# One-hot rows of a graph kernel's gate stage, written as four-byte words in two passes

## The reference, cut to what matters

```python
ei = emb[atom_z[src]]
ej = emb[atom_z[dst]]
gate = gate + (ei * (ej @ adapt)).sum(-1, keepdims=True)
msg = gate * h[dst] * (cw * mj)[:, None]
agg = jax.ops.segment_sum(msg, src, num_segments=N)
```

## Time and profile before

| | us |
|---|---|
| median of three runs | 5722.47 |
| lowest, highest | 5720.83, 5742.07 |
| the profiled execution | 5716.15 |
| its span | 5714.5 |
| the gate stage in it, some 1201 to 1871 | 670 |

### The profile page before, as it was taken

One profiled execution on the slowest core, in us unless ns is written; L12 is line 12 of the kernel. 1 busy time (PEld: TensorE's weight loads), 2 busy tenths in 40 slices (PEclk: granted clock), 3 DMA queues, 4 the chain that ended last, 5 costly groups with the idle time before them and its releaser, 6 DMA issues. The chain is left out here.

```text
span 5714.5 us, 186702 instructions
## 1 busy us (share of the span) xinstructions
PE 4266.2 (75%) x79491; PEld 3587.6 (63%) x79576; DVE 3792.0 (66%) x7929; ACT 2244.4 (39%) x7754; POOL 2676.4 (47%) x2702
## 2 busy tenths in 40 slices
PE   6888884036666499859976997699757844978887
PEld 3555542035665389848875887588636733977786
DVE  6888875069999588667766875677585446545244
ACT  3333331036666255535543554455402424101310
POOL 2777777756666177627752775367421510000000
PEclk7766665569889699979987998799787977988897
DMA  9322222257676344344424442444155443000000
GB/s 353 79 74 73 69 68 65 53 130 205 191 203 184 115 156 155 111 109 164 155 93 122 167 158 74 137 163 166 55 103 211 146 120 110 2 9 4 4 4 10
DMA packets 480761, 652.89 MB, mean 114 GB/s; under 512 B 315713, under 2 KB 362949, under 8 KB 476694
## 3 DMA queue, kind: packets, MB, share of 16 engines
q1 hardware_dynamic: 443541, 591.08, 33.0%
q0 software_dynamic: 33856, 48.44, 3.5%
q10 hardware_dynamic: 2496, 0.98, 0.1%
HBM read 460.24 MB, written 180.09 MB: 112 GB/s over the span
## 5 line engine op out<-in xcount | busy, mean ns | idle before, releaser
L299 POOL DMA_INDIRECT edges<-sb_bk_rec,sb_bk_pos x782 | 783.5, 1002 | 324.9 <-issue 235.0
L1718 ACT ACTIVATE sb_at_val<-banks,sb_at_prob 128x49 f32<-128x49 f32 x3800 | 772.2, 324 | 189.9 <-PE banks L1654 182.4
L1757 DVE TENSOR_REDUCE sb_at_tops<-banks 128x1 f32<-128x512 f32 x1000 | 653.3, 662 | 275.7 <-PE banks L1634 272.9
L1610 PE MATMUL banks<-sb_near,sb_at_hotT_d 128*128 128x49 bf16 x11100 | 609.8, 184 | 36.4 <-issue 18.6
L1612 PE MATMUL banks<-sb_queryp,sb_at_hotT_s 128*128 128x49 bf16 x11400 | 624.3, 185 | 14.1 <-issue 13.9
L1570 POOL TENSOR_TENSOR sb_at_key<-sb_at_key,sb_at_attr 128x400 f32<-128x400 f32 (+1 forms) x400 | 371.3, 929 | 498.2 <-ACT sb_at_key L1702 487.2
L1610 PEld LDWEIGHTS banks<-sb_near,sb_at_hotT_d 128*128 128x128 fp8e4 x11100 | 559.8, 96 | 41.5 <-issue 34.5
L1612 PEld LDWEIGHTS banks<-sb_queryp,sb_at_hotT_s 128*128 128x128 fp8e4 x11400 | 559.8, 96 | 17.1 <-issue 17.0
L1577 POOL TENSOR_TENSOR sb_at_val<-sb_at_val 128x490 f32<-128x490 f32 (+1 forms) x400 | 386.7, 967 | 68.3 <-ACT sb_at_val L1718 66.8
L1579 POOL TENSOR_TENSOR sb_at_val<-sb_at_val 128x490 f32<-128x490 f32 (+1 forms) x400 | 386.1, 965 | 31.3
L1654 PE MATMUL banks<-sb_near,sb_at_hotT_d 128*128 128x49 bf16 x11100 | 358.8, 186 | 35.7 <-ACT sb_at_val L1718 22.6
(11 more groups left out here) (695 smaller groups left out, 10114.5 us busy)
## 6 DMA issues: line engine op xcount, KB each, us to landing
sb_at_attr<-attr SPq DMA_DIRECT2D x100, 760.0 KB, 7.5
sb_at_hotT_s<-rows_src_t SPq DMA_DIRECT2D x100, 608.0 KB, 5.2
sb_at_hot_s<-rows_src SPq DMA_DIRECT2D x100, 608.0 KB, 8.7
sb_at_hotT_d<-rows_dst_t SPq DMA_DIRECT2D x100, 592.0 KB, 6.1
edges<-sb_pad SPq DMA_DIRECT2D x95, 460.0 KB
sb_gt_rec<-edges SPq DMA_DIRECT2D x25, 1748.0 KB
sb_we_hotT<-rows_dst_t SPq DMA_DIRECT2D x52, 592.0 KB, 5.7
attr<-sb_gt_rec SPq DMA_DIRECT2D x25, 760.0 KB, 12.7
```

The costliest lines, as they stand in the source:

```text
L299: pool.indirect_dma_start(list1, bass.IndirectOffsetOnAxis(pos[:, t:t + 1], 0), rec[:, k, j, :], None).then_inc(sent[k], 16)
L1610: pe.matmul(ps[:, 0, H1 * j:H1 * j + H1], where, what, start=(n == 0), stop=(n == 2))
L1718: ins = act.mul(val[:, v % VB, j, 0, :], ps[:, 5, H1 * j:H1 * j + H1], prob[:, i % 2, k:k + 1])
L1757: dve.tensor_reduce(tops[:, i % 2, g:g + 1], ps[:, 3 + x % 2, 0:P * len(RG[g])], AX, ALU.max).then_inc(s_top, 1)
```

## The change

Four fp8 numbers fill one 32-bit word, so a row of 128 columns is 32 words. Only one of them isn't zero, and its value is the fp8 one (56) moved to one of four bytes. `at_nodes` works out each place's quarter (its number divided by four) and its word's value (from the number's last two bits), in four more instructions that each wait for the one before. A piece is then made by two instructions: `same_quarter` compares 32 numbers with the place's quarter and writes bf16 zeros and ones into `same` (two buffers), and `one_hots` multiplies these with the word, read as fp32, and writes int32 into the memory of the one-hots. `same_quarter` stands in the unit where the comparison stood, ahead of `message(u)`; `one_hots` stands behind `message(u)`. What is written for PE and the stores is byte for byte what it was.

```diff
-                dve.tensor_scalar(ls[:, at, :], rec[:, i % HB, :, R_SRC], -float(P * i), None, ALU.add).then_inc(s_at, 1)
-                dve.tensor_tensor(ld[:, at, :], rec[:, i % HB, :, R_DST], starts, ALU.subtract).then_inc(s_at, 1)
+                dve.tensor_scalar(loc[:, 0, :], rec[:, i % HB, :, R_SRC], -float(P * i), None, ALU.add).then_inc(s_at, 1)
+                dve.tensor_tensor(loc[:, 1, :], rec[:, i % HB, :, R_DST], starts, ALU.subtract).then_inc(s_at, 1)
...
+                link(dve.tensor_scalar(byte[:], loc[:], 3, None, ALU.bitwise_and))
+                link(dve.tensor_scalar(word[:, at], byte[:], float(2 ** 26), float(531 * 2 ** 21), ALU.mult, ALU.add))
+                link(dve.tensor_scalar(loc[:], loc[:], 2, None, ALU.arith_shift_right))
+                link(dve.tensor_copy(quarter[:, at], loc[:]))
...
-                dve.tensor_tensor(to[:, i % HB, a:b, :], along(c["iota"][:], b - a), bc(loc[:, i % 2, a:b], P), ALU.is_equal,
-                                  saturate=False).then_inc(s_hot, 1)
...
+                    dve.tensor_tensor(same[:, m % 2, 0:b - a, :], along(c["iota"][:, 0:W4], b - a),
+                                      bc(quarter[:, i % 2, v, a:b], W4), ALU.is_equal).then_inc(s_same, 1)
...
+                    dve.wait_ge(s_same, m + 1)
+                    to = (hot_s if side == "s" else hot_d)[:, i % HB, a:b, :].bitcast(I32)
+                    dve.tensor_tensor(to, same[:, m % 2, 0:b - a, :], bc(word[:, i % 2, v, a:b].bitcast(F32), W4), ALU.mult
+                                      ).then_inc(s_hot, 1)
...
-            for n in range(NM):
-                one_hot(0, n)
+            for n in range(0, NM, 2):
+                same_quarter(0, range(n, n + 2))
+                one_hots(0, range(n, n + 2))
...
-                        for n in MAKE_AT[q]:
-                            one_hot(i + 1, n)
+                        same_quarter(i + 1, MAKE_AT[q])
                     message(u)
+                    if i + 1 < NB:
+                        one_hots(i + 1, MAKE_AT[q])
```

More of the change, by code:

```diff
@@ L1237, in gate_edges @@
     rec = m.sb("gt_rec", [P, HB, KT, REC])
-    ls, ld = m.sb("gt_ls", [P, 2, KT]), m.sb("gt_ld", [P, 2, KT])
+    W4 = P // 4
+    loc, byte = m.sb("gt_loc", [P, 2, KT], I32), m.sb("gt_byte", [P, 2, KT], I32)
+    quarter, word = m.sb("gt_quarter", [P, 2, 2, KT]), m.sb("gt_word", [P, 2, 2, KT], I32)
+    same = m.sb("gt_same", [P, 2, 12, W4], BF16)
     hot_s, hot_d = m.sb("gt_hot_s", [P, HB, KT, P], F8), m.sb("gt_hot_d", [P, HB, NW, P], F8)
@@ L1247, in gate_edges @@
     names = ["near", "at", "hot", "turned", "copied", "rows", "emb", "prod", "msg", "rest", "split2", "sum", "added",
-             "link", "second", "back"]
+             "link", "second", "back", "same"]
     with stage(nc, "gate", *names, *[f"rec{k}" for k in range(HB)], *[f"outh{k}" for k in range(HB)], "outt0", "outt1",
@@ L1251, in gate_edges @@
             block, s_near, s_at, s_hot, s_turned, s_copied, s_rows, s_emb, s_prod, s_msg, s_rest, s_split2, s_sum,
-            s_added, s_link, s_second, s_back, *dmas):
+            s_added, s_link, s_second, s_back, s_same, *dmas):
         s_rec, s_outh, s_outt, s_outa, s_far = dmas[0:3], dmas[3:6], dmas[6:8], dmas[8:11], dmas[11:15]
@@ L1429, in at_nodes, with same_quarter, one_hots @@
                 dve.tensor_tensor(w1[:, i, :], rec[:, i % HB, :, R_W1], dead[:, i, :], ALU.add).then_inc(s_at, 1)
[L1431 to L1436, removed]
-                dve.tensor_tensor(to[:, i % HB, a:b, :], along(c["iota"][:], b - a), bc(loc[:, i % 2, a:b], P), ALU.is_equal,
-                                  saturate=False).then_inc(s_hot, 1)
+                link(dve.tensor_scalar(byte[:], loc[:], 3, None, ALU.bitwise_and))
+                link(dve.tensor_scalar(word[:, at], byte[:], float(2 ** 26), float(531 * 2 ** 21), ALU.mult, ALU.add))
+                link(dve.tensor_scalar(loc[:], loc[:], 2, None, ALU.arith_shift_right))
+                link(dve.tensor_copy(quarter[:, at], loc[:]))
+            def same_quarter(i, ns):
+                for n in ns:
+                    side, a, b = MAKE[n]
+                    m, v = NM * i + n, "sd".index(side)
+                    if m >= 2:
+                        dve.wait_ge(s_hot, m - 1)
+                    dve.tensor_tensor(same[:, m % 2, 0:b - a, :], along(c["iota"][:, 0:W4], b - a),
+                                      bc(quarter[:, i % 2, v, a:b], W4), ALU.is_equal).then_inc(s_same, 1)
+            def one_hots(i, ns):
+                for n in ns:
+                    side, a, b = MAKE[n]
+                    m, v = NM * i + n, "sd".index(side)
+                    if n == 0 and i >= HB:
+                        dve.wait_ge(s_outh[i % HB], 32 * (i // HB))
+                        dve.wait_ge(s_sum, Q * (i - HB + 1))
+                    dve.wait_ge(s_same, m + 1)
+                    to = (hot_s if side == "s" else hot_d)[:, i % HB, a:b, :].bitcast(I32)
+                    dve.tensor_tensor(to, same[:, m % 2, 0:b - a, :], bc(word[:, i % 2, v, a:b].bitcast(F32), W4), ALU.mult
+                                      ).then_inc(s_hot, 1)
             def message(u):
```

## The result

The changed kernel takes 6182.8 us (median of four runs, 6180.1 to 6190.0) where the kernel before takes 5724.4 (median of four), a ratio of 1.079 with a 95% interval of 1.078 to 1.081. The forecast was 6142, with a range of 6010 to 6200.

The account below looks back on a forecast made before the run. A one-unit ring through PE, ACT and DVE was to bound the gate stage: 38.8 us a block plus 0.75 x 6.7 for the clock gives 43.8 against 26.3; 24 blocks add 420, plus 2 once: 6142 us, range 6010 to 6200.

Parts of the forecast that it names:

- Part 1, the ring of one unit: Gate stage: piece finished behind its message, so PE, ACT and DVE wait in turn each unit; 38.8 us a block against 26.3.
- L: Gate stage: way from a finished piece through PE to the end of ACT's multiplications; 3.03 to 3.82 us at 2.4 GHz.
- my 2.6: Lower end of the forecast wait of DVE's message for ACT in nearly every gate-stage unit, some 2.6 to 4 us.
- Part 2, the product: DVE's two short passes for one long: product 0.41 to 0.59 us on the ring; bounds -30 and +60 us in all.
- sign of failure: Gate-stage pieces: the prediction was to fail if the two-pass piece took over 1 us.
- Part 3, the nodes' step: Four more instructions in `at_nodes`, 0.9 us a block, hidden in q = 0's wait: cost 0, except 2 us once.
- The clock: PE's granted clock in the gate stage: three quarters of units at 1.2 GHz, raising a block from 38.8 to 43.8 us.
- the possible 6.7: Extra us a gate-stage block if PE's clock were 1.2 GHz throughout, 45.5 against 38.8.
- first rival, the low clock in every unit: Gate stage: PE's pauses return the clock to half in every unit, 45.5 us a block, 6185 us; chance 0.19.
- The rival on the other side: Gate stage: DVE's work alone sets the pace, so shorter pieces save 4.4 us a block, 105 us: 5617; chance 0.04.

Follow-up runs that it names:

- the kernel with the product early and short splits: The changed kernel with the product ahead of message(u) and POOL splitting only one row of each message, other rows' remainders left out: 5676.6 us, ratio 0.990.
- The other one-pass kernels: The kernel before with its comparison behind the message (6366.0 us), with PE's turns behind its rows (5722.5), or with POOL's splits cut to one row (5680.3).
- the other two-pass kernels: The changed kernel with product ahead of message (5717.6 us), turns behind rows (5682.9), both (5661.2), idle matmuls (6056.0), or product ahead and splits cut to one row (5676.6).
- the early product: The changed kernel with the product right behind its comparison, ahead of message(u): 5717.6 us, ratio 0.997.

## Why the prediction was right

The forecast missed the median by 41 us. Some 26 of these lie in the stage, 16 outside it, and 2 are a slip in my last addition, since 6138 + 6 is 6144 and not 6142. Some 4 went the other way: the median of the changed kernel stands 2 us above its profiled execution (6180.6), where I took 6 from the kernel before. The mechanism held; that the total came so near owes something to terms that made up for each other, named below.

**Part 1, the ring of one unit.** Right, as the mechanism and in place. It showed in the waits (35 us became 504), in the timeline (each message behind its piece), and in two edits that each opened the ring at another place. L came out as read from the trace of before: at the low clock 4.03 and 4.49 us in the changed kernel, where the earlier trace rows had 4.04 and 4.48, and at the high clock 3.03 and 3.58 in the one with the idle matmuls, as in the earlier trace rows. The message's idle time was 3.1 us on average; only in q = 0 it was 2.2, under my 2.6, because the nodes' step fills part of it.

**Part 2, the product.** I took 0.41 us for 256 elements and 0.55 for 384. The rows have 0.42 and 0.55. The 1.05 ns an element and 0.14 us fixed, from comparisons written as fp8, hold for a product written as int32. For the block's last two products I took 0.59 us and they took 0.98, as the second ran beside POOL's split. That was luck: the turns of the first go on meanwhile, so L behind the second was 3.40 us at the high clock and not 3.82, and the sum of the two, 4.38, is what I had (4.41). The comparisons took 0.82 us on average where I allowed 0.6 at most, most likely because POOL's splits run beside them (0.48 in the kernel with the product early and short splits); it cost nothing, since they lie in L. Both passes of a piece together take 1.33 us, over the 1 us that I named as a sign of failure; but only the product stands on the ring, so the sign was badly chosen.

**Part 3, the nodes' step.** Hidden, as said: it lies in q = 0's wait. Counted from the step's first instruction, block 1's first piece ended 2.0 us later than before (3.93 us against 1.93), and that instruction itself started 2.0 us later (1226.06 against 1224.06), when the transfer of its records had landed.

**The clock, the term that was mis-sized.** The clock of the stage was 0.62, so about three quarters of the time was at 1.2 GHz, as I assumed. But it isn't the share of the time that counts: it is whether the turns and the rows are at the low level. Taken only from each piece's end to the end of its multiplications, over 168 units, the granted clock was 0.57, and 0.72 in the rest of the ring. Not one of these 168 stretches was at the high level throughout, and 73 were at the low level throughout. So PE got the higher level more often where it had little to do. The means of L in the seven units sum to 29.7 us, against 24.1 in the kernel with the idle matmuls: 5.6 us of the possible 6.7, where I had 5.0. The other part of the miss isn't the clock: the block with the idle matmuls is 39.3 us and not 38.8. Of the 44.9 - 43.8 = 1.1 us a block, 26 us in all, some 0.6 are the clock's and 0.5 small excesses in the other terms, the way L above all (20.7 us in q = 1 to 6 at the high clock, where I had 20.4). With both the forecast would have been 6170.

The prediction's first rival, the low clock in every unit with 6185, has a number nearer to the measured one, but not by its mechanism: it asks for 45.5 us a block and the block was 44.9, between the two, and the rest is the 16 us outside the stage. The rule of the Trainium skill beside it ("TensorE: Matmul & The Clock Gate", section "HAM oscillation — how this bites in real kernels"), by which each pause makes the next step start cold, agrees with this trace in many units and not in all: the clock was 0.50 in 1598 to 1604 us, but 95 of the 168 stretches were partly at the high level.

**What is left.** The stage accounts for 448 us of the 464 between the two spans: the instruction after the stage that adds to `nodes` starts at 1901.5 before and at 2349.3 after. The other 16 lie in the attention layers, whose code isn't touched. From that instruction to the last maximum of these layers it is 2172 us in the kernel before and 2188 in the changed one. The other one-pass kernels have 2181, 2182 and 2185, and the other two-pass kernels 2183 to 2193. So most of the 16 appears within the one-pass form too, and goes with the execution or with when the layers start; a share that goes with the two-pass form isn't ruled out. The cause stays open.

**The rival on the other side** was right on one point: DVE does have less to do, and where the ring is open that shows, 2.3 us a block. My price for it, 4.4 a block, left POOL's collisions out of the two-pass form's cost. The rule of the Trainium skill, "VectorE: DVE Perf Modes", in its section on the errata, by which bf16 data copied as int32 halves the elements and the time, agrees in its basis: 384 words took 0.55 us where the same 1536 bytes as fp8 took 1.75. But that is the product alone; the comparison in front of it costs the same again.

**My largest miss among the experiments** was the early product (5635 forecast, 5717.6 measured). I had put the comparison and the product at 0.55 each into the ring and compared with a block that holds collisions. What is on a ring has to be taken with its neighbours' disturbance from both kernels, or from neither.

## What to carry to other kernels

Where engines wait for each other by turns, cost a move by the ring and not by busy time: list the instructions from a result to the next one that needs it, across all engines' fixed orders, and count how many units the ring spans. Moving an instruction from ahead of a wait to behind it can halve that number, and here an instruction that got three times shorter then cost 8% of the kernel. Before giving up a shorter form, look for another place to open the ring; here the turns behind the rows and the product ahead of the message gave 1.3% over the kernel before.

## What the runs show of the hardware

Useless work on TensorE made the kernel faster: 36 idle matmuls a unit lifted the granted clock from 0.62 to 0.98 and took 127 us off. That holds for this loop, in which PE has a pause of some 3 us in each unit.

DVE's instructions on SBUF and POOL's hold each other up, and the one that starts second takes longer. The product of 384 words took 0.55 us in the timeline of the changed kernel, where POOL's split starts behind it, and 0.92 with the product early, where the split was already running. POOL's first split took 1.40 us on average beside DVE's long comparisons and 0.75 beside the short ones; DVE's product took 0.72 us on average with the product early and the long splits, and 0.48 with the short ones. The message's instructions with an input in `banks` (PSUM) kept their times in all these kernels, 0.33 and 0.436 us.
